# Inverse scales split by their upper 16 bits, scales and clips in a new order, and the last products in two output banks from the second tile on

## The reference

```python
def layernorm(x): return (x - mean(x)) / sqrt(var(x) + 1e-5)

def bit_linear(x, w, b):
    gamma_x = clip(max(abs(x), axis=-1), 1e-5)              # one per token
    x_dq = clip(round(x * 127 / gamma_x), -128, 127) * gamma_x / 127
    gamma_w = clip(mean(abs(w)), 1e-5)                      # one per matrix
    w_dq = clip(round(w / gamma_w), -1, 1) * gamma_w
    return x_dq @ w_dq.T + b

q, k = ctx @ Wq.T + bq, ctx @ Wk.T + bk                     # per batch, 256 x 128
x = x + layernorm(x)-rows mixed by softmax(q @ k.T)
h = layernorm(x)
x = x + bit_linear(silu(bit_linear(h, gate_w, gate_b)) * bit_linear(h, val_w, val_b), out_w, out_b)
```

## Time and profile before

| | us |
|---|---|
| median of 3 runs | 61.09 (60.72 to 61.1) |
| the profiled execution | 60.99 |
| its span, first to last instruction | 59.3 |
| PE busy | 51.3 (87%) |
| DVE busy | 48.2 (81%) |
| ACT busy | 47.6 (80%) |
| POOL busy | 44.9 (76%) |

### The profile page before, as it was taken

The page is one execution under the profiler, slowest core; times in us unless marked ns, Lnnn a source line. Parts: engine busy times, 40 slices in busy tenths (PEclk is TensorE's granted clock), DMA queues, the critical chain, the costliest instruction groups (busy, mean ns, idle before and its releaser), DMA issues.

```text
span 59.3 us, 1140 instructions
## 1 busy us (share of the span) xinstructions
PE 51.3 (87%) x298; PEld 32.7 (55%) x301; DVE 48.2 (81%) x122; ACT 47.6 (80%) x84; POOL 44.9 (76%) x102
## 2 busy tenths in 40 slices
PE   1999998899999699929899988899999997979910
PEld 1768866468888478613323634333473752759800
DVE  3249859897999799996998989898999997997150
ACT  0723929989999999979999685999999999798700
POOL 4970002798789888798779978989999999999900
DMA  0789999999993000000002001299270199920573
GB/s 0 161 232 369 409 339 409 408 407 411 397 400 136 0 17 0 0 6 0 6 0 44 0 0 32 57 180 174 51 137 0 31 185 178 242 72 0 176 235 120
DMA packets 11070, 8.92 MB, mean 150 GB/s; under 512 B 7605, under 2 KB 9141, under 8 KB 11065
## 3 DMA queue, kind: packets, MB, share of 16 engines
q1 hardware_dynamic: 10912, 8.72, 47.5%
q10 hardware_dynamic: 152, 0.14, 1.3%
HBM read 6.04 MB, written 1.05 MB: 120 GB/s over the span
## 4 chain that ended last, share of the span: by engine, by line
POOL 30%; PE 26%; issue 17%; DVE 12%; ACT 9%; POOLq 0%; ACTq 0%
POOL h L344 6%; PE psO L940 5%; PE psT L753 5%; POOL r_cols L276 4%; PE psV L763 3%; DVE nmax L467 3%; PE psG L763 3%; PE psH L940 3%; PE psT L778 3%; POOL rstd L311 3%; ACT o_early L723 3%; DVE x L485 3%; POOL pgam L325 2%; POOL res L372 2%; POOL w_int L409 2%
## 5 line engine op out<-in xcount | busy, mean ns | idle before, releaser
L572 DVE TENSOR_REDUCE pmax<-prod 128x1 f32<-128x1024 f32 x8 | 9.7, 1210 | 0.1
L707 ACT ACTIVATE sil<-psG,s_gv 128x1024 f32<-128x1024 f32 x8 | 8.9, 1112 | 0.6 <-PE psG L874 0.2
L556 DVE TENSOR_TENSOR prod<-psV,sil 128x1024 f32<-128x1024 f32 x7 | 8.5, 1221 | 0.9 <-ACT sil L707 0.5
L859 PE MATMUL psG<-ter_gate,hT 128*128 128x512 bf16 x31 | 8.0, 378 | 0.8 <-ACT sil L707 0.7
L886 PE MATMUL psV<-ter_val,hT 128*128 128x512 bf16 x26 | 7.0, 381 | 0.2 <-issue 0.2
L940 PE MATMUL psO<-ter_out,pT 128*128 128x256 bf16 x48 | 6.2, 273 | 0.7 <-ACT o_early L723 0.7
L940 PEld LDWEIGHTS psO<-ter_out,pT 128*128 128x128 bf16 x48 | 4.4, 98 | 2.4 <-DVE pT L599 0.8
L281 POOL TENSOR_SCALAR ve<-mv 128x2 f32<-128x2 f32 (+1 forms) x3 | 0.6, 197 | 6.0 <-DVE mv L463 5.9
L694 ACT ACTIVATE hT<-psH,unshift 128x256 bf16<-128x256 f16 x8 | 3.8, 475 | 1.5 <-PE psH L842 1.4
L859 PEld LDWEIGHTS psG<-ter_gate,hT 128*128 128x128 bf16 x32 | 2.7, 96 | 4.0 <-issue 2.0
L644 ACT ACTIVATE prob<-psT,nmax 128x256 f32<-128x256 f32 x8 | 3.7, 479 | 1.1 <-DVE nmax L467 1.1
(11 more groups left out here) (142 smaller groups left out, 144.9 us busy)
## 6 DMA issues: line engine op xcount, KB each, us to landing
w_gate<-in_w_gate SPq DMA_DIRECT2D x2, 512.0 KB, 5.1
x<-in_x_tok SPq DMA_DIRECT2D x4, 256.0 KB, 6.3
w_val<-in_w_val SPq DMA_DIRECT2D x2, 512.0 KB, 7.2
xt_sb<-in_x_T SPq DMA_DIRECT2D x4, 256.0 KB, 7.8
w_out<-in_w_out SPq DMA_DIRECT2D x2, 512.0 KB, 8.9
out_x<-res SPq DMA_DIRECT2D x8, 128.0 KB, 1.8
ctx_sb<-in_ctx_T SPq DMA_DIRECT2D x2, 128.0 KB, 2.8
ctx_sb<-in_ctx_T SPq DMA_DIRECT2D x1, 256.0 KB, 6.0
```

The lines of the kernel that those rows point to most:

```text
L556: nc.vector.tensor_tensor(prod[:, t % P_RING, :], psV[:], sil[:, t % S_RING, :], ALU.mult).then_inc(prod_done, 1)
L572: nc.vector.tensor_reduce(pmax[:, t:t + 1], prod[:, t % P_RING, :], AX.X, ALU.max, apply_absolute_value=True).then_inc(pmax_done, 1)
L707: nc.scalar.activation(sil[:, t % S_RING, :], psG[:], ACT.Silu, scale=s_gv[:, t, 0:1]).then_inc(sil_done, 1)
L859: nc.tensor.matmul(psG[:, c * HC:(c + 1) * HC], hT[:, t, k, :], w_ter[0][:, k * HID + c * HC:k * HID + (c + 1) * HC], start=(k == 0), stop ...
```

## The change

Five things change.

First, the digits. r_gv gets a third axis of NPART. The upper 16 bits of an f32, seen as bf16, are its first digit (`r_top`), so the digit is read out of r_gv itself: for each of the two further digits one subtraction, and then copies that put all three digits into r_cols, nine columns at a time. On POOL that is two subtractions and two copies, before it was five instructions; r_rest is gone. gmin becomes a step of its own, `smallest_p(g)`, with its own semaphore. For group 0 DVE does it, in a new `inverse_parts` of two subtractions and one copy.

```diff
             def inverse_parts(g):
...
-                same(part[0], whole).then_inc(r_step[g], 1)
-                pool.wait_ge(r_step[g], 1)
-                nc.gpsimd.tensor_tensor(rest, whole, part[0], ALU.subtract).then_inc(r_step[g], 1)
...
+                for i in range(NPART - 1):
+                    if i:
+                        pool.wait_ge(r_step[g], i)
+                    nc.gpsimd.tensor_tensor(r_gv[:, a:e, :, i + 1], r_gv[:, a:e, :, i], r_top[:, a:e, :, i],
+                                            ALU.subtract).then_inc(r_step[g], 1)
+                pool.wait_ge(r_step[g], NPART - 1)
...
+                for q in range(2):
+                    same(cols[:, :, q, :].rearrange("p n (j i) -> p n j i", i=NPART),
+                         top.to_broadcast([P, 2 * (e - a), NPART, NPART])).then_inc(r_step[g], 1)
...
+            def smallest_p(g):
...
+                pool.wait_ge(rgv_done, g + 1)
+                nc.gpsimd.tensor_scalar(gmin[:, a:e], r_gv[:, a:e, 1, 0], -GAMMA_MIN, 1.0 / QMAX, ALU.mult,
+                                        ALU.mult).then_inc(gmin_done, 1)
...
+                nc.vector.tensor_copy(cols.rearrange("p n q (j i) -> p n q j i", i=NPART),
+                                      top.to_broadcast([P, 2 * (e - a), 2, NPART, NPART])).then_inc(r_step[g], 2)
```

```diff
-        ALT = 5
+        ALT = 1
         ps_o = [psH[:, 0:D] if t >= ALT and t % 2 else psO[:, 0:D] for t in range(T)]
...
-            gate(6); biases(6); value(6); last_product(1); gate(7); biases(7); last_product(2); value(7);
+            gate(6); biases(6); value(6); last_product(1); gate(7); biases(7); value(7); last_product(2);
```

More of the change, by code:

```diff
@@ L203, in xattn_ffn @@
         psT_h = [psT[:, i, :].bitcast(F16) for i in range(2)]
+        r_top = r_gv[:].bitcast(BF16).rearrange("p t w (i two) -> p t w i two", two=2)[:, :, :, :, 1]
         h_h = h[:].bitcast(F16).rearrange("p t (n two) -> p t n two", two=2)[:, :, :, 0]
@@ L420, in _ @@
             add_bias(1); centre_x2(0); centre_x2(1); std_x2(0); std_x2(1); h_step(0); gamma_h(0); h_step(1);
[L421 to L428, removed]
+            gamma_h(1); h_round(0); h_round(1); h_round(2); inverse_parts(1); smallest_p(0); smallest_p(1);
+            centre_x2(4); h_round(3); centre_x2(6); centre_x2(7); std_x2(2); add_bias(2); h_step(2); gamma_h(2);
+            h_round(4); h_round(5); gamma_p(0); h_round(6); inverse_parts(2); smallest_p(2); gamma_p(1);
+            p_round_int(0); add_bias(3); gamma_p(2); h_round(7); to_int(2, 0); to_int(2, 1); gamma_p(3);
+            shift_x(); add_bias(4); scale_out(0); add_bias_shift(5); gamma_p(4); p_round_int(3); scale_out(1);
+            p_round_int(5); scale_out(2); add_bias_shift(6); add_residual(0); scale_out(3); p_round(6);
+            scale_out(4); scale_out(5); scale_out(6); add_bias_shift(7); add_residual(1); add_residual(2);
+            scale_out(7); add_residual(3); add_residual(4)
         @block.vector
@@ L531, in scales_h, with inverse_parts @@
                 dve.wait_ge(sgv_done, g + 1)
-                nc.vector.reciprocal(r_gv[:, a:e, :], s_gv[:, a:e, :]).then_inc(rgv_done, 1)
+                nc.vector.reciprocal(r_gv[:, a:e, :, 0], s_gv[:, a:e, :]).then_inc(rgv_done, 1)
+            def inverse_parts(g):
+                a, e = GROUPS[g]
+                dve.wait_ge(rgv_done, g + 1)
+                dve.wait_ge(c_fill, 5)
+                for i in range(NPART - 1):
+                    if i:
+                        dve.wait_ge(r_step[g], i)
+                    nc.vector.tensor_tensor(r_gv[:, a:e, :, i + 1], r_gv[:, a:e, :, i], r_top[:, a:e, :, i],
+                                            ALU.subtract).then_inc(r_step[g], 1)
+                dve.wait_ge(r_step[g], NPART - 1)
+                cols = r_cols[:, a:e, :].rearrange("p t (w q c) -> p (t w) q c", w=2, c=32)[:, :, :, 0:KB]
+                top = r_top[:, a:e].rearrange("p t w i -> p (t w) i").unsqueeze(2).unsqueeze(3)
+                nc.vector.tensor_copy(cols.rearrange("p n q (j i) -> p n q j i", i=NPART),
+                                      top.to_broadcast([P, 2 * (e - a), 2, NPART, NPART])).then_inc(r_step[g], 2)
             def gamma_w(w):
@@ L612, in _ @@
             mean_x2(2); stats_x2(3); gamma_w(1); mean_x2(3); centre_x2(2); h_max(0); h_max(1); scales_w(1);
[L613 to L621 removed]
+            h_inv(0); h_inv(1); scales_h(0); inverse_parts(0); scales_h(1); add_x(4); add_x(5); clip(0, 1);
+            stats_x2(4); stats_x2(5); mean_x2(4); mean_x2(5); clip(1, 0); add_x(6); clip(1, 1); add_x(7);
+            stats_x2(6); stats_x2(7); mean_x2(6); mean_x2(7); times_value(0); h_max(2); p_max(0); h_inv(2);
+            times_value(1); scales_h(2); p_max(1); times_value(2); invert_gamma_p(0); p_max(2);
+            invert_gamma_p(1); gamma_w(2); times_value(3); scales_w(2); invert_gamma_p(2); p_max(3);
+            times_value(4); clip(2, 0); clip(2, 1); p_max(4); times_value(5); invert_gamma_p(3); p_max(5);
+            invert_gamma_p(4); widen(2); gamma_p(5); invert_gamma_p(5); times_value(6); p_max(6); gamma_p(6);
+            invert_gamma_p(6); widen(3); times_value_half(0); times_value_half(1); p_max(7); gamma_p(7);
+            invert_gamma_p(7); p_round_half(0); p_copy(6); add_residual(5); add_residual(6); add_residual(7)
         @block.scalar
```

45 lines of the change are left out of this document (14 added, 31 removed).

## The result

The changed kernel took 63.11 us (median of 4 runs, 63.01 to 63.5) against 61.06 before: 1.038 times as long, 95% interval 1.034 to 1.043. A second set of runs, unaltered, is among the experiments: 62.93 against 61.06, 1.031 (1.025 to 1.037). The medians by themselves divide to 1.034; a ratio given with an interval is an estimate from the fast runs alone. The forecast was 62.2 with a range to 62.8. The direction was right; the loss was 1.9 to 2.1 us and not 1.2.

The account below looks back on a forecast made before the run. DVE was taken to bound the middle and POOL, with SP's stores queued behind its adds, the end. Front -0.1 and end +1.3 gave +1.2 on 61.09, 62.3, taken as 62.2 for cheaper s_o; range 61.1 to 62.8.

Parts of the forecast that it names:

- What bounds the kernel: DVE in the middle, within 8% of its floor; POOL in the last stretch, with SP's stores waiting for its adds.
- the second rival: POOL paces the middle, so its removed work comes off: -0.85 us, or 60.2 us; chance 0.12.
- The front, -0.1: From tile 2 on, the products shift by -0.1 us, between -0.5 and +0.4, after the digits move to DVE.
- the price of the digits on DVE: Group 0's two subtractions and one copy on DVE, about 0.2 us apart: 3 x 0.2 = 0.6 us.
- 34.74: Predicted start in us of times_value(2) on DVE, against 34.85 before.
- POOL's h_step(2): New wait near 31.85 us, 0.2 us ahead of the h_inv(2) queued before times_value(1); if late, all DVE is.
- The cast: DVE's widen(3) beside a POOL add: 0.2 us of contention in both lists, cancelling; by the lock rule +0.2 more.
- POOL's end, +1.3: POOL gains p_round_int(5), gives away gamma_p(6), and ends at 57.3 us; with queued stores the span grows 1.3.
- the fourth rival: POOL's tail does not bind, s_o being cheaper: saves 0.4 us at most, 61.8; counted within the forecast's 0.6 chance.
- The stores behind it: SP's stores 5, 6 and 7 queue behind store 4 at 0.37 us each, so store 7 goes at 58.4 us.
- The matmul chain: PE's last matmuls start about 0.3 us sooner with the second output bank; this -0.3 is hidden behind the stores.
- the third rival: POOL's list ahead of h_step(2) ends 0.5 us later, holding DVE's products: +1.7, 62.8 us; chance 0.11.

Follow-up runs that it names:

- the run with s_o(3) ahead: The changed kernel with scale_out(3) ahead of add_residual(0) on POOL, so DVE's widen(3) starts before that add; ratio 1.027 to the kernel before.
- The new end alone: The kernel before with only the changed list ends: POOL's new order with p_round_int(5), gamma_p(6) on DVE, ALT = 1; 62.45 against 60.82 us, 1.025.
- the first batched version: The kernel before with the changed end, POOL's eight s_o batched into fewer products, adds ahead of later bias work, stores reordered; ratio 1.006.
- The second bank alone: The kernel before with only ALT = 1, the second output bank used from tile 1 on; ratio 1.000.
- the probes: The kernel before plus three digit instructions on DVE on scratch data; first start to next instruction 0.52 us with POOL idle, 0.87 beside POOL's passes.

## Why the prediction missed

The end was right in mechanism and nearly in size. The front was taken for a small gain and was a loss of half a microsecond. By the prediction's own steps:

- **What bounds the kernel** (DVE the products, POOL the end, SP's queue behind POOL): right. With the new front, POOL lost 1.7 us of digits and the products came later all the same; with the digits back on POOL they came sooner. The chain of waits, which had POOL in the middle, was not the bound, so the second rival (60.2 us) is refuted.
- **The front, -0.1**: wrong, it was +0.56 at tile 2 and +0.45 at tile 5. This is the step that failed. Its term that was mis-sized is the price of the digits on DVE, 0.6 us, with 0.2 for the copy; they took 1.09. The 0.2 was right for a DVE that is alone (0.20 measured). What the step missed is that POOL's three h_round run beside it. The 0.92 beside the 0.70 of POOL's adds was a sign that the two engines slow each other, and I used it for POOL alone and priced DVE by its short rows. The error is 0.49 of the 0.67 us by which tile 2 is behind its 34.74; with the digits on POOL it comes 0.50 sooner. Smaller errors stand beside it. DVE's list up to times_value(0) was summed to 28.46 and then put at 28.65, with 0.19 us for which no term is given; it ran to 29.10, so 0.16 us more are other instructions of the list. From times_value(0) to (1) it is 3.58 for 3.51: POOL's h_step(2), the step named as a new wait, ended at 32.56 instead of 31.85, and h_inv(2) starts at 32.59, so it now decides, but by less than 0.1 us. From (1) to (2) it is 2.73 for 2.59, since value(2) waits for psV. The prediction had this limit, 34.8, in its next sentence, and still took 34.74; against 34.85 that limit leaves hardly a gain at tile 2.
- **The cast**: the prediction let the 0.2 us of contention cancel, since a cast and an add overlap in both lists. It did not ask which of them starts first. Before, the cast was ahead by 0.08 and the add paid 0.22; after, the add is ahead by 0.01 and the cast pays 0.56. The page named in the prediction, the Trainium skill's "SBUF — State Buffer", section "Who interferes with whom", has the rule in the general form, that whoever issues first holds the pair for its whole instruction and the other fully blocks. The traces agree with the order in three cases, and in after in the direction that I had not considered, DVE behind POOL. They agree with the size only in part: the cast lost 0.56 us where the add still had 0.72 to run, the s_o of the run with s_o(3) ahead lost 0.24 of 0.44, and the add of the kernel before 0.22 of 0.35. This last one the prediction had misread: the cast was 0.08 us ahead, so by the rule the add would have stood for 0.35 us and not for all of 0.43, and the sum would have been larger by 0.13 and not by 0.2. The run without the long cast won 0.19 us of the span and moved POOL's last add, behind which the stores queue, by 0.08; the other 0.35 us of its gain on DVE did not reach the end.
- **POOL's end, +1.3**: right. From p_round_int(5) to the last add the sum had 10.65 us, it took 10.51 (47.16 to 57.67), so 0.14 of the 0.4 us of the fourth rival came. The new end alone gave +1.5 from times_value(2) on, for +1.3. The difference is the next point.
- **The stores behind it, 3 x 0.37 = 1.11**: too small, 1.35. Only one distance had been read, that from store 4 to 5; the next are 0.47 and 0.50. The landing behind the last, 2.21, was 2.25.
- **The matmul chain, -0.3, hidden**: hidden it was, but a gain of 0.3 us shows in no run. From times_value(7) to the end of DVE's last add it takes 6.89 us for 7.18, only because the long cast makes times_value(7) late by about as much: counted from times_value(2) it is 22.24 for 22.21. With the short cast times_value(7) does come the 0.2 us sooner that the prediction gave it (14.81 for 15.03 behind times_value(2)), but the last add on DVE is only 0.08 sooner there (22.13), and 0.14 in the first batched version (22.07). The second bank alone moved the wait to widen(5).
- **The sum.** Forecast 60.5 for the span (59.3 + 1.2). POOL's last add was expected at 57.2 with the front's -0.1 and came at 57.67, 0.47 later. The front makes 0.54 of it (the rounding of tile 3 at 45.27, where -0.1 put it at 44.73), the wait ahead of p_round_int(5) 0.07, and POOL's list takes 0.14 off. Behind it come 0.03 us from the add to the issue of store 4, 0.24 for the stores and 0.04 for the landing. 60.5 + 0.78 is 61.28, for 61.3 in the trace.
- **The chances**: 0.68 for slower was right. The range ended at 62.8 because only the near edge of the third rival was taken in; its size was nearly met, though not by its mechanism alone (a late h_step(2)) but by the digits. The forecast's own side was bounded by +0.4 for the front, too narrow for a copy of which no row existed and whose upper bound I had put at 0.48 without letting it work: with the copy at 0.48 the front would have been +0.2, with all three instructions at 0.48 it would have been +0.7, and +0.56 lies between.

## What to carry to other kernels

A small instruction on an engine that a neighbour can hold up is not priced by its shortest row: look at what its neighbour runs in those microseconds, and take both lengths into the range. When outputs leave through one queue in a fixed order, the last one costs its issue time for every row that waits behind the latest one; find which engine finishes last, and either let its rows go out last or let it finish first. Taking a wait away, as with the second bank, is worth only the distance to the next wait, here that for ACT's widen(5): it was worth nothing.

## What the runs showed of the hardware that I had not expected

DVE waits for POOL as well as the other way round. A copy of 72 bf16 numbers per partition took 0.20 us with POOL idle and 0.40 to 0.47 beside POOL's one-input passes of 128 x 256; a cast of 1024 numbers, 0.43 otherwise, took 0.99 when POOL's two-input add had started 0.01 us earlier, and POOL's s_o took 0.58 for 0.34 when the cast had started 0.01 us earlier. The subtractions of 128 x 4 were less affected in the probes, 0.37 against 0.46 for two; in the changed kernel one of them took 0.22 and the other 0.43. The five instructions that took longer there than alone all ended 0.01 to 0.06 us behind the end of one of POOL's passes. A rounding of 128 x 512 on DVE took 0.92 us for 0.48 when it started 0.09 us behind a two-input add of POOL. Another took 1.03 for 0.49 although it started 0.03 us ahead of such an add; there the add before it still had 0.06 us to run, and in the changed kernel a rounding that started at 53.77, 0.02 us before such an add ended, took 0.48. So the order of two starts does not tell it alone, and what decides within some hundredths of a us was not settled. SP's issue of a 128 KB store takes 0.33 to 0.51 us in the changed kernel, and 0.38 to 0.50 pass from one to the next when several are queued.
